# Zero products on TensorE in the landmark softmax stage: four narrow ones at each batch's turn, and round the last column sums

## The reference, cut to what matters

```
attn2 = softmax(einsum('bhid,bhjd->bhij', q_l, k_l), -1)   # landmarks against landmarks
col = max(abs(a).sum(-1)); row = max(abs(a).sum(-2))       # one number each over all batches
z = swapaxes(a, -1, -2) / (col * row)                      # start of the pseudo-inverse
for _ in range(6):
    az = a @ z
    z = 0.25 * z @ (13 I - az @ (15 I - az @ (7 I - az)))
```

## Time and profile before

| | |
|---|---|
| median of 3 runs | 731.64 us |
| profiled execution, its time | 736.04 us |
| its span (first to last instruction) | 734.2 us |
| mean granted TensorE clock | 0.939 of full |
| TensorE busy | 681.5 us, 93% |
| VectorE, ScalarE, GpSimd busy | 56%, 51%, 31% |
| landmark stage | from 36.4 to 84.5 us of the span |

### The profile page before, as it was taken

The page is one execution under the profiler, slowest core; times in us unless marked ns, Lnnn a source line. Parts: engine busy times, 40 slices in busy tenths (PEclk is TensorE's granted clock), DMA queues, the critical chain, the costliest instruction groups (busy, mean ns, idle before and its releaser), DMA issues. The chain is left out here.

```text
span 734.2 us, 15178 instructions
## 1 busy us (share of the span) xinstructions
PE 681.5 (93%) x6033; PEld 527.5 (72%) x6033; DVE 413.5 (56%) x843; ACT 377.6 (51%) x1035; POOL 229.7 (31%) x204
## 2 busy tenths in 40 slices
PE   9887898999999999999889999869999999989896
PEld 5676798988989898988785555557666666647555
DVE  3457347667575767674525333426777777764322
ACT  4656447565655647473246555335555455544531
POOL 4155325343544344444300434023222222201001
PEclk9997699999999999999958999957999999996999
DMA  8200000000000000000000000000000000000000
GB/s 267 99 3 1 1 1 3 2 1 2 1 2 2 2 1 3 2 1 2 1 1 1 1 1 1 1 1 1 1 1 1 1 2 1 1 1 1 1 15 17
DMA packets 5214, 8.23 MB, mean 11 GB/s; under 512 B 3608, under 2 KB 4120, under 8 KB 4760
## 3 DMA queue, kind: packets, MB, share of 16 engines
q1 hardware_dynamic: 4552, 7.20, 3.1%
q10 hardware_dynamic: 592, 0.07, 0.1%
HBM read 6.71 MB, written 0.55 MB: 10 GB/s over the span
## 5 line engine op out<-in xcount | busy, mean ns | idle before, releaser
L977 POOL TENSOR_TENSOR STD<-STD,NN 91x492 f32<-91x492 f32 (+1 forms) x96 | 104.0, 1101 | 149.2 <-DVE NN L1106 78.7
L677 PE MATMUL PS<-ST 128*91 128x123 f32 x768 | 92.9, 272 | 4.8 <-DVE ST L1112 4.6
L1106 DVE SCALAR_TENSOR_TENSOR NN<-ST,PS 91x492 f32<-91x492 f32 x96 | 62.9, 661 | 56.3 <-PE PS L677 56.3
L677 PE MATMUL PS<-NN 128*91 128x123 f32 (+1 forms) x768 | 89.6, 268 | 3.2 <-DVE NN L1106 3.2
L677 PEld LDWEIGHTS PS<-ST 128*91 128x91 f32 x768 | 83.5, 159 | 11.0 <-DVE ST L1112 7.1
L677 PEld LDWEIGHTS PS<-NN 128*91 128x91 f32 x768 | 82.2, 160 | 10.4 <-DVE NN L1106 6.4
L1746 PE MATMUL PS<-QR,KA 128*128 128x270 f32 x256 | 72.2, 413 | 0.0
L895 ACT ACTIVATE STD<-ST 91x492 f32<-91x492 f32 (+1 forms) x96 | 51.6, 569 | 39.6 <-DVE ST L1112 39.6
L1860 DVE TENSOR_SCALAR CL<-PS,K 128x270 f32<-128x270 f32 x144 | 65.7, 496 | 9.8 <-PE PS L1746 4.5
L1112 DVE SCALAR_TENSOR_TENSOR ST<-PS,STD 91x492 f32<-91x492 f32 (+1 forms) x96 | 55.9, 599 | 22.1 <-POOL STD L977 12.4
L1801 ACT ACTIVATE EX<-CL,NG 128x540 f32<-128x540 f32 x64 | 46.7, 741 | 32.8 <-DVE CL L1860 32.7
(11 more groups left out here) (326 smaller groups left out, 1250.5 us busy)
## 6 DMA issues: line engine op xcount, KB each, us to landing
TP<-taps SPq DMA_DIRECT2D x1, 1204.0 KB, 16.1
MA<-mat SPq DMA_DIRECT2D x1, 1120.0 KB, 7.5
MF<-mat SPq DMA_DIRECT2D x1, 1024.0 KB, 12.6
WI<-wide SPq DMA_DIRECT2D x1, 902.0 KB, 9.0
CO<-const SPq DMA_DIRECT2D x1, 512.0 KB, 15.7
MQ<-mat SPq DMA_DIRECT2D x1, 512.0 KB, 16.4
out<-OS SPq DMA_DIRECT2D x8, 45.0 KB
XA<-xpatch SPq DMA_DIRECT2D x1, 256.0 KB, 2.8
```

The lines of the kernel that those rows point to most:

```text
L677: last = nc.tensor.matmul(PS[0:NL, PINV + q, h % 4 * SW + c0:(h % 4 + 1) * SW], x[:, h, 0:NL], x[:, h, c0:SW], start=True, stop=True)
L977: nc.gpsimd.tensor_tensor(TD[:, 4 * q:4 * q + 4, c0:SW], SA[:, 4 * q:4 * q + 4, c0:SW], NN[0:NL, 4 * q:4 * q + 4, c0:SW], ALU.subtract).th ...
L1106: v.scalar_tensor_tensor(out=NN[0:NL, own, :], in0=ST[0:NL, b % 2, own, :], scalar=N_S, in1=heads4(PS[0:NL, PINV + q, 0:4 * SW]), op0=ALU. ...
```

## The change

`spin` becomes a helper of the whole program and gets a second form. With `low=96` it issues products of 128 rows by 32 columns of zeros with 256 moving columns, in plain float32, into partitions 96 to 127 of a bank; `bank` is SCORES, which is 0. ZK is allocated for the whole program. Four such products stand at the end of each of the 8 turns, four more behind the loop, four between `sums(6)` and `sums(7)`, and two behind `weigh(0)`: 42 in all. None of them waits for a semaphore, none posts one. The products of the first block stay as they were.

```diff
+        ZK = sb("ZK", [128, 512], F32R)
...
+        def spin(n, bank=7, low=0):
+
+            for _ in range(n):
+                if low:
+                    nc.tensor.matmul(PS[low:128, bank, 0:256], ZK[:, 0:128 - low].bitcast(F32), ZK[:, 0:256].bitcast(F32),
+                                     start=True, stop=True)
+                else:
+                    nc.tensor.matmul(PS[:, bank, :], ZK[:, 0:128], ZK[:, :], start=True, stop=True)
...
-        ZK = ts("ZK", [128, 512], F32R)
...
-        SPIN = 7
...
-                def spin(n):
-
-                    for _ in range(n):
-                        nc.tensor.matmul(PS[:, SPIN, :], ZK[:, 0:128], ZK[:, :], start=True, stop=True)
...
                         ALONG[i](0)
                     if i + 1 < B // 2:
                         proj(i + 1, 1)
+                    spin(4, SCORES, 96)
+                spin(4, SCORES, 96)
                 sums(B - 2)
+                spin(4, SCORES, 96)
                 sums(B - 1)
                 weigh(0)
+                spin(2, SCORES, 96)
                 pe.wait_ge(sem("n_diag"), 1)
```

## The result

The changed kernel takes 747.87 us (median of 4 runs, 745.00 to 751.07), against 731.58 for the kernel before. The ratio is 1.0215, with a 95% interval of 1.0179 to 1.0250. It is slower, by 13 to 18 us. The forecast was 741.5 with a range of 734 to 750: the side and the range held, and the size was short by 6.4 us. The forecast was also a change within 2%: this interval has 2% inside it, so on which side of 2% the change lies is open. Measured once more, beside other runs of the kernel before, it is 746.39 against 733.13, a ratio of 1.0187 (1.0153 to 1.0221), 13.3 us.

A forecast was written before the change was run, and what follows sets the result against it. The landmark stage was taken as close to bound by TensorE, with half clock costing something. Products 18.3, less 1.4 absorbed, 8.1 and 1.5 given back, plus 2.6 lost, make 9.9 on 731.64: 741.5 us, range 734 to 750.

The forecast's parts named there:

- The price of a product: On TensorE, each zero product takes 0.435 us, 18.3 us for 42; estimated from column sums it would be 0.48.
- What lies beside other work: In the landmark stage, TensorE's waits absorb 2.8 us of zero products, less 1.4 for a new wait: 1.4 us.
- No overlap: Zero products and the scores behind them do not run together; the overlap rival gave 738 us, chance 0.13.
- The new wait: Ahead of line 594, TensorE would newly wait 1.4 us for batch 0's exponentials of turn 4.
- The transposes' waits: TensorE's waits of 1.38 and 1.67 us ahead of the two transposes stay, coming from ScalarE's own chain.
- The fall at the transposes: The clock falls again at the two transposes, as at 74.0 us before; 0.9 to 3.5 us lost, 2.6 taken.
- the rise within the eight: The clock rises inside or at the end of the eight zero products behind the transposes, 0.87 us each at half speed.
- The sum for the stage: Over the landmark stage and L659 just beyond it, all costs and gains net to 9.9 us longer.
- what the clock gives back: At full clock up to `start(0)`, work is shorter by 8.1 us, and L659 beyond the stage by 1.5.
- The last rival: Clock dips beyond the stage decide the time, plus or minus 4 us on any case; chance 0.04.
- the case in which narrow products don't count: Narrow products on TensorE are no activity for the clock: 18.1 us slower, 750 us, range 747 to 757; chance 0.17.
- the chain through VectorE and ScalarE sets the turn: Faster rival: in the turns TensorE only follows scores to maxima to exponentials, zero products lie in waits; 728 us, chance 0.06.

The follow-up runs named there:

- 64-column: The changed kernel with 64 moving columns in place of 256 in each of its 42 products; 733.95 us, ratio 1.0022.
- bfloat16 version: The changed kernel with its 42 products in bfloat16 in place of float32, 256 moving columns as before; 734.73 us against 731.46, ratio 1.0041.
- The kernel before's second profile: The kernel before, without an edit, run and profiled again; 731.20 us.
- the one without products: The changed kernel without any of its 42 narrow products, keeping the zero tile's new place; 732.14 us against 733.02, ratio 0.9983.
- turns only: The changed kernel with only the 32 products at the ends of the turns; 738.62 us, ratio 1.0085.
- behind the loop only: The changed kernel with only the 10 products behind the loop (4, 4 and 2); 733.90 us, ratio 1.0019.
- waits filled: In place of the changed kernel's 42 products, 22 of 256 columns where TensorE would wait; 734.69 us, ratio 1.0024.
- without the last two: The changed kernel without the two products behind `weigh(0)`, so 40; 743.83 us against 731.46, ratio 1.0158.
- with two more: The changed kernel with four products behind `weigh(0)` instead of two, so 44; 744.85 us against 731.46, ratio 1.0179.
- the pair of filled waits: 22 products at TensorE's waits, with 256 moving columns (734.69 us, ratio 1.0024) or with 2 (732.53 us, ratio 0.9990).

## Why the prediction was right, and where it was short

*The price of a product* was 0.435 us and is 0.46 ahead of scores and 0.43 ahead of column sums. The other bound, 0.48 from the column sums, is above both. At the full clock the 42 come to about 19.0 us and not 18.3: seven groups ahead of scores at 1.84, the rest at 0.43 to 0.48 each. The 64-column and the bfloat16 version confirm what the price consists of. The 0.12 us that a group ahead of scores costs beyond one ahead of column sums comes again there (0.57 against 0.45, and 0.54 against 0.43).

*What lies beside other work* was 1.4 us. Of the 3.4 us of waits ahead of scores and column sums that the prediction listed, 1.2 are left (0.64 and 0.59) and 1.27 are new, so it is 0.9.

*No overlap*: right. Scores start 0.06 to 0.07 us before the zero products' recorded end, each time. Scores(4) start at 65.89 where the prediction named 60. That 60 was a slip: four groups of 1.74 behind 54.97, less 0.53 of waits, give 61.4 by its own terms. The other 4.5 us are, to 0.2, the 1.8 by which the stage starts later and the 2.9 of turn 0's dip.

*The new wait*, 1.4 us, is 1.27. *The transposes' waits* stay to the hundredth. *The fall at the transposes* came at 85.1 and *the rise within the eight* at 91.9. The prediction took 2.6 us for what this takes; the eight took 5.56 us instead of 3.7, 1.9 more, and the second transpose 0.64: 2.5.

*The sum for the stage* was 9.9. From the first trace to the second, with 1.8 ahead of the stage and 2.9 of turn 0 set aside, turns, end and batch 0 are 9.8 + 4.2 - 1.4 - 2.9 = 9.7 us longer. That it agrees to 0.2 us is in part luck. The kernel before's second profile and the one without products have the same dip in turn 0 as the changed kernel, and from them to it the same three stretches are 11.2 and 11.1 us longer. The mechanism holds, to about 1.5 us.

*The terms that were short* are the products' time and, as much, what the clock gives back. The spans and mean clocks of all runs show it. A span times its share of missing clock is about what half speed cost; the remainder is what the work and its waits would take at the full clock. It is an estimate, since a wait at the half clock is counted half to either side. Against the runs of the kernel before in the same round, in means, which differ a little from the medians:

| kernel | whole difference | at the full clock | by the clock |
|---|---|---|---|
| changed, second measurement | +13.3 | +18.7 | -5.3 |
| turns only | +6.3 | +15.1 | -8.9 |
| behind the loop only | +0.9 | +5.3 | -4.5 |
| waits filled | +1.4 | +8.2 | -6.8 |
| without the last two | +11.6 | +18.6 | -7.0 |
| with two more | +13.2 | +19.7 | -6.5 |
| 64 columns | +1.0 | +6.4 | -5.4 |
| bfloat16 | +3.2 | +6.1 | -2.9 |

The prediction had +16.9 for the products and -7.0 for the clock (8.1 and 1.5 given back, 2.6 taken again). So 1.8 us are missing on the products' side and 1.7 on the clock's, together, but for rounding, the 3.4 us between 9.9 and 13.3. The table also says why the parts don't add up. At the full clock they nearly do, 15.1 and 5.3 against 18.7. But alone they gain 8.9 and 4.5 us by the clock, and together 5.3. Each of the clock's figures is uncertain by about 1 us. Where in the program the whole kernel loses that gain is not shown.

*The last rival*, "the clock's dips elsewhere decide", got 0.04 and 4 us to either side. In the profiles the dips ahead of the products make 4.7 us and the stretch behind the attention up to 5.5. Those are no cost of the change: the kernel before and the one without products show such dips too. The first figure, 16.3 us, has two of its four runs in the group above 750 us, the second, 13.3, one of seven.

*The range* held the first figure by luck. 747.87 lies above the forecast's own 738.5 to 745; the second difference, 13.3 on 731.64, would be just inside. The range reached 750 because it took in the lower part of the case in which narrow products don't count (747 to 757), and that is not what happened.

*The rivals.* That narrow products don't count as activity falls with the pair of filled waits, 256 columns against 2, one profile each. That the chain through VectorE and ScalarE sets the turn falls with the turns: TensorE had hardly a wait left between 48.6 and 70.1 us. The faster side had one true thing in it. At the transposes, where TensorE waits 1.4 and 1.7 us, products are free, and the stage gets shorter, by 2.5 us in one version and 3.4 at its end in another. At the other waits the profile doesn't separate what the products cost from what the clock gave. And neither median moved.

*What stays open*: why a stage 2 to 3 us shorter brings nothing in the median of 12 runs. In the profiles part of it goes into a longer dip in batch 0 (42.4 instead of 40.8 us in both versions). By the table above, the version with filled waits paid 8.2 us at the full clock for 6.8 of clock. Open too is why the gain by the clock is smaller with all 42 products than with its parts. Both would need many profiles of one kernel; each here has one or two.

## What to carry to other kernels

A filler instruction is free only where its engine waits, and it holds everything behind it in the list: count the waits at the full clock first, put fillers into them with a size to match, and never ahead of the operation that starts the next turn's chain. Cheaper fillers held the clock less well here (of those in the turns only float32 products of 256 columns, 0.46 us each, kept it at 1.00), but they lost far less time: 0.8 us with 64 columns and 3.3 in bfloat16, against 13.3. None gained. And before a few microseconds of gain or loss are believed, cut several profiles of the same kernel at the same instructions, and see by time and mean clock whether the profiled execution is like the others: here a stretch that nobody had touched moved by 5.5 us, and both profiles of the changed kernel were of its slowest runs.

## What the runs showed of the hardware

- 22 narrow products of 256 columns kept the granted clock at 1.00 from 57 to 82 us, where 22 of 2 columns at the same places left it at a mean of 0.65 from 57 to 86 (one profile each). These products had 32 of 128 output columns and data of zeros.
- A float32 product of 128 rows by 32 columns with 256 moving columns takes 0.43 us at 2.4 GHz ahead of products of the same strip and 0.46 ahead of scores of 32 rows by 96 columns; a bfloat16 one takes 0.11 and 0.135. A group of four costs 0.11 to 0.13 us more ahead of scores, in float32, in bfloat16 and with 64 columns alike; the two shapes never overlapped.
- Where the clock falls is not a property of the kernel alone. The kernel before had its first dip at 57 us in one profile and at 20 us in another, and the same stretch of 1825 recorded matmuls took between 287.0 and 292.5 us.
- A gain in clock can be followed by a loss: a stage shortened by 2.5 us was followed by a dip of 6.8 us instead of 3.4, in one profile.
- The clock fell in stretches with no wait longer than 1.7 us: at 56.9 us behind waits of 0.33 and 1.15 us in the kernel before, and at 85.1 behind 1.38 in the changed kernel, with TensorE busy 6.50 of the 9.00 us ahead.
